# Chunk work of VectorE ahead of a step's maximum in the first cross-attention, and the added one of the silu on ScalarE

## The chip, the core and the metric

The kernel runs on one core of a Trainium2 chip. The metric is the device time of one execution in microseconds (us). Engines: TensorE (PE; its weight loads are shown as PEld), VectorE (DVE), ScalarE (ACT), GpSimd (POOL), SyncE (SP), which issues the DMAs. Each engine takes its instructions strictly in the order in which they are written; engines wait for each other on semaphores.

## What is computed

A decoder of two layers over x of 4 x 1024 x 256: self-attention, cross-attention to 154 context rows and a feed-forward network in each, every one with a residual and a layer norm behind it. The change lies in the stretch that computes the cross-attention of layer 0 and, beside it, the front half of layer 0's feed-forward for two of the four batch entries:

```python
# cross-attention of layer 0: 16 heads of 64
q = (Q @ Wq.T + bq).reshape(n, lq, H, D);  k, v likewise from the context
scores = jnp.einsum('nqhd,nkhd->nqkh', q, k) / jnp.sqrt(jnp.float32(D))
attn = jax.nn.softmax(scores, axis=2)
out = jnp.einsum('nqkh,nkhd->nqhd', attn, v)
x = _layernorm(x + out @ Wo.T + bo)
# feed-forward of layer 0
h = bit_linear(x, w1)                       # rows scaled and rounded
h = depthwise_conv1d(h.transpose(0, 2, 1), conv_w, conv_b)   # 3 taps
h = jax.nn.silu(h.transpose(0, 2, 1))
return bit_linear(h, w2)                    # needs each row's largest |h|
```

The silu is computed from the halved convolution c (taps and bias are halved ahead): silu = (tanh(c) + 1) * c.

## The kernel before

**Steps.** The cross-attention is a loop of 128 steps m. A step covers 128 query rows and 4 heads; four steps in a row (m mod 4 = 0, 1, 2, 3) share one set of queries. In this text r0, r1, r2, r3 name steps by m mod 4, and four steps from r3 to r2 are a group. In a step each engine does its part, in this order:

- TensorE: scores(m) into psA (L1025); transposes(m-2) of the normalised weights pr into psB (L1039 of four heads, L1041 of the rest), of which the first part waits until VectorE has copied out that of the step before; in r0 and r1 the queries of the next set; in r2 the output projection (16 matmuls, L978, wo_x); in r3 weights times values (L1056, L1061); and side work (transposing x, keys, values of the next entry) in some of the steps r0 and r1.
- VectorE: copy_transposes(m-3) (L1368, L1371), maxima(m) (L1377, waits for the scores), in r3 the residual (L1397, waits for the projection; TensorE's values wait for it), normalise_rows(m-1) (L1384, L1387, L1389), in r3 the statistics, in r0 the layer norm (L1409), and then the chunk work.
- ScalarE: the four exponentials of step m (L1242, wait for the maximum), its copies out of PSUM (queries L1183 in r0 and r1, values L1189 in r3), and then the chunk work.
- GpSimd: the inverse deviation (L1312, L1313), the bias of the next half (L1305, in every fourth r2), the rounding of x, and the chunk work.

**Chunks.** The hidden layer of 1024 features is done for two entries in 16 chunks of 128 features (128 partitions) x 1024 rows. Chunk i begins at step 61 + 4i, an r1: `chunk_from(m, n)` gives the chunk that began n steps before m. Its path through the engines before the change, with the steps behind its first (0 is r1, 1 is r2, 2 is r3, 3 is r0):

| offset | engine | operation | line |
|---|---|---|---|
| 0, 1 | TensorE | first layer, half 0 at the end of r1, half 1 within r2 | L978 |
| 0, 1 | VectorE | rescale of half 0, half 1, PSUM to hw | L1437 |
| 2 | ScalarE | outer_taps: the first tap into cvw, the third into yw | L1214, L1218 |
| 3 | VectorE | middle_tap, added to cvw | L1443 |
| 3 | GpSimd | add_tap: cvw = cvw + yw | L1290 |
| 5 | ScalarE | tanh of cvw into yw | L1222 |
| 5 | GpSimd | silu: yw = yw + 1, then yw = yw * cvw | L1294, L1295 |
| 7 | SyncE | store of yw to DRAM | L943 |
| 7 | ScalarE | absolute value into cvw | L1226 |
| 8 | VectorE | take_max: running maximum ymw over chunks, all 1024 columns | L1454 |

hw, cvw and yw have two buffers, so chunk i+2 takes those of chunk i. After each entry's last chunk ymw is transposed on TensorE (L1104, task ym) and reduced on VectorE (scale_hidden, L1462); for the second entry that stands at the end of the block. psO has two banks, given to TensorE's tasks in turn in the order in which they are written (C_SLOT).

## Time and profile before

| | us |
|---|---|
| median of 3 runs | 2543.93 |
| lowest and highest | 2537.71, 2546.5 |
| the profiled execution's own time | 2538.13 |
| its span, first to last instruction | 2536.2 |
| steps 0 to 60 (no chunk; steps by the start of their maximum) | 262.1 |
| steps 61 to 124 (16 groups, all with a chunk) | 364.5 |
| busy in the span: PE, DVE, ACT, POOL | 84%, 59%, 47%, 29% |

The whole span's shares mix stages with other limits. Only the stretch from 892 to 1564 us, the cross-attention, is touched, and of it mainly the 364.5 us with chunks.

### The profile page before, as it was taken

To read this page: it belongs to the slowest core of one execution; us is meant where nothing else is said; L and a number is where in the kernel's file an instruction comes from. 1 tells how busy PE (TensorE), PEld (TensorE's weight loads), DVE (VectorE), ACT (ScalarE), POOL (GpSimd) and SP (SyncE) were. 2 spreads that over 40 slices of the span, in tenths; PEclk is the share of its full clock that TensorE was granted. 3 is DMA by queue.
4 is the path that set the end of the run, shared out by engine and by line. 5 is a ranking of instruction groups with operands and counts; after the bars stand their busy time and mean duration, and the time that the engine had idled before them with its cause. 6 is when DMAs were issued, how large, how long until landed. Compare 5 with 4: busy or idle time off the path is not lost. (4 is left out here: it accounts for less than half of the span.)

```text
span 2536.2 us, 32771 instructions
## 1 busy us (share of the span) xinstructions
PE 2121.4 (84%) x11586; PEld 1190.8 (47%) x11586; DVE 1499.2 (59%) x2813; ACT 1180.7 (47%) x2629; POOL 740.4 (29%) x773
## 2 busy tenths in 40 slices
PE   6888888888888689998878875789899977788886
PEld 3333343344342345565555444556566643444444
DVE  5564565466564266666876885484836344557655
ACT  2345534534535255555655661466642314354342
POOL 4251310220010100122543444264723222343232
PEclk8899999999999899999999998999999978899898
DMA  7335333432421100001010003110001156544311
GB/s 158 98 55 139 75 63 74 89 73 59 69 46 43 62 20 5 26 26 34 32 46 24 32 32 139 61 40 9 28 13 62 36 115 121 114 94 88 71 54 42
DMA packets 132500, 156.56 MB, mean 62 GB/s; under 512 B 36477, under 2 KB 102913, under 8 KB 132242
## 3 DMA queue, kind: packets, MB, share of 16 engines
q1 hardware_dynamic: 132338, 154.47, 25.6%
q8 instruction: 94, 1.54, 0.3%
q14 instruction: 68, 0.56, 0.1%
HBM read 107.55 MB, written 46.86 MB: 61 GB/s over the span
## 5 line engine op out<-in xcount | busy, mean ns | idle before, releaser
L530 ACT ACTIVATE pbuf_sb<-psB 128x512 f32<-128x512 f32 (+1 forms) x608 | 331.0, 573 | 336.7 <-PE psB L409 312.9
L716 DVE TENSOR_REDUCE negm_sb<-psA 128x1 f32<-128x768 f32 (+6 forms) x352 | 347.1, 1022 | 136.8 <-PE psA L397 134.4
L1242 ACT ACTIVATE pw_sb<-psA,nmx_sb 128x154 f32<-128x154 f32 x512 | 192.4, 390 | 219.1 <-DVE nmx_sb L1377 219.0
L406 PE MATMUL psB<-qst_sb,kst_sb 99*128 99x512 bf16 (+3 forms) x768 | 235.1, 336 | 42.7 <-ACT pbuf_sb L530 34.6
L395 PE MATMUL psA<-kst_sb,qst_sb 96*128 96x512 bf16 (+3 forms) x768 | 200.5, 340 | 34.9 <-DVE negm_sb L716 29.9
L1377 DVE TENSOR_REDUCE nmx_sb<-psA 128x4 f32<-128x616 f32 x128 | 101.8, 795 | 142.5 <-PE psA L1025 142.5
L423 PE MATMUL psO<-pbuf_sb,V_sb 128*32 128x512 f32 (+3 forms) x1536 | 168.8, 513 | 8.8 <-ACT OT_sb L516 7.4
L406 PEld LDWEIGHTS psB<-qst_sb,kst_sb 99*128 99x128 bf16 x768 | 75.0, 99 | 180.7 <-ACT pbuf_sb L530 146.9
L2879 DVE TENSOR_REDUCE negm_sb<-psA 128x2 f32<-128x320 f32 x256 | 115.7, 480 | 71.0 <-PE psA L2646 65.9
L2766 ACT ACTIVATE pb_sb<-psB 128x512 f32<-128x512 f32 x160 | 92.8, 601 | 137.1 <-PE psB L2656 135.1
L1039 PE MATMUL psB<-ident_sb,pr_sb 128*128 128x128 f32 x512 | 85.0, 290 | 66.0 <-DVE pt_sb L1368 65.9
L395 PEld LDWEIGHTS psA<-kst_sb,qst_sb 96*128 96x128 bf16 x768 | 61.0, 100 | 159.4 <-DVE negm_sb L716 98.7
L2016 PE MATMUL psO<-va_sb,pat_sb 128*128 128x256 f32 x512 | 118.1, 384 | 9.9 <-DVE pat_sb L2446 9.9
L978 PE MATMUL psO<-XT_sb,wq_x_sb 128*128 128x512 f32 x256 | 124.2, 610 | 0.0
L978 PE MATMUL psO<-wo_x_sb,ox_sb 128*128 128x256 f32 x512 | 122.1, 395 | 2.0 <-DVE hw_sb L1437 1.2
L2646 PE MATMUL psA<-kst_sb,qst_sb 97*128 97x160 bf16 x512 | 83.3, 251 | 46.6 <-DVE negm_sb L2879 40.9
L1387 DVE TENSOR_TENSOR pr_sb<-pw_sb,prx_sb 128x512 f32<-128x512 f32 x128 | 118.3, 924 | 4.4
L2419 DVE TENSOR_REDUCE nma_sb<-psA 128x1 f32<-128x1024 f32 x32 | 39.1, 1222 | 138.2 <-PE psA L2016 138.2
L2016 PE MATMUL psA<-qa_sb,ka_sb 128*128 128x512 f32 x256 | 115.1, 592 | 0.0
L567 POOL TENSOR_TENSOR OT_sb<-OT_sb,rden_sb 128x1024 f32<-128x1024 f32 x15 | 35.3, 2354 | 270.9 <-DMA rden_sb<-dens_dram 270.9
L2016 PEld LDWEIGHTS psO<-va_sb,pat_sb 128*128 128x128 f32 x512 | 97.8, 192 | 33.8 <-DVE pat_sb L2446 13.8
L978 PEld LDWEIGHTS psO<-wo_x_sb,ox_sb 128*128 128x128 f32 x512 | 101.4, 200 | 19.5 <-issue 2.2
(308 smaller groups left out, 4495.9 us busy)
## 6 DMA issues: line engine op xcount, KB each, us to landing
qst_sb<-parts_dram SPq DMA_DIRECT2D x192, 128.0 KB, 4.6
rden_sb<-dens_dram SPq DMA_DIRECT2D x128, 128.0 KB, 2.7
parts_dram<-parts_sb SPq DMA_DIRECT2D x32, 384.0 KB, 3.1
kst_sb<-parts_dram SPq DMA_DIRECT2D x96, 128.0 KB, 7.5
x_dram<-X_sb SPq DMA_DIRECT2D x64, 128.0 KB, 1.7
y_dram<-yw_sb SPq DMA_DIRECT2D x16, 512.0 KB, 2.6
Y_sb<-y_dram SPq DMA_DIRECT2D x16, 512.0 KB, 8.4
parts_dram<-partsb_sb SPq DMA_DIRECT2D x16, 384.0 KB, 3.1
```

The lines of the kernel that those rows point to most:

```text
L395: nc.tensor.matmul(psA[:, k, at + lo:at + hi], qst[0:QK_ROWS, gg % 3, h, j * P:(j + 1) * P], kst[0:QK_ROWS, gg % 3, h, lo:hi], start=True, ...
L406: last = nc.tensor.matmul(psB[:, k, at:at + hi - lo], kst[0:MAX_ROWS, gg % 3, h, i * P:(i + 1) * P], qst[0:MAX_ROWS, gg % 3, h, lo:hi], st ...
L423: last = nc.tensor.matmul(psO[32 * h:32 * h + 32, c, lo - c * 512:hi - c * 512], V[:, b % 2, i, at:at + 32], pbuf[:, i % 2, h, lo:hi], sta ...
L530: nc.scalar.activation(pbuf[:, key % 2, heads[0]:heads[-1] + 1, lo:hi], psB[:, (nb.n - 1) % 2, 0:len(heads) * (hi - lo)] .rearrange("p (h ...
L716: nc.vector.tensor_reduce(out=negm[:, gg % 2, heads[0]:heads[-1] + 1, j], in_=psA[:, (na.n - 1) % 2, :].rearrange("p (h n) -> p h n", h=le ...
L978: last = nc.tensor.matmul(dst, lhsT(i), rhs(i), start=(i == 0), stop=(i == n - 1))
L1242: last = nc.scalar.activation(pw[:, m % 2, h, :], psA[:, m % 2, at:at + K], ACT.Exp, bias=nmx[:, m % 2, h:h + 1], accum_out=psx[:, m % 3, ...
L1377: nc.vector.tensor_reduce(out=nmx[:, m % 2, :].rearrange("p (b a) -> p a b", a=2), in_=psA[:, m % 2, :].rearrange("p (a n) -> p a n", a=2) ...
L1387: nc.vector.tensor_tensor(pr[:, q % 3, 0:4, :], pw[:, q % 2, :, 0:P], prx[:, q % 3, :].unsqueeze(2).broadcast_to([P, 4, P]), ALU.mult)
L2016: last = nc.tensor.matmul(dst, lhsT(i), rhs(i), start=(i == 0), stop=(i == n - 1))
L2766: nc.scalar.activation(pb1[:, v % 2, h, :], psB[:, (nb.n - 1) % 2, :], ACT.Exp).then_inc(b_free, 1)
L2879: nc.vector.tensor_reduce(out=negm1[:, gg % 2, 2 * half:2 * half + 2, j], in_=psA[:, 0, half * 512:half * 512 + 2 * KP].rearrange("p (a n) ...
```

## The change

On VectorE the chunk work stands between copy_transposes(m-3) and maxima(m) instead of at the step's end, one step later: the rescales at offsets 1 and 2, the middle tap at 4. take_max is split into halves of 512 columns, at offsets 9 and 11; each adds one to max_taken, so that the waits on it count double. On ScalarE outer_taps is split: first_tap stays at offset 2, last_tap goes to 3; tanh is followed by an Identity activation with a bias of one, which waits for the tanh by a semaphore; absolute goes to offset 8 and to the end of the step. On GpSimd add_tap goes to offset 4 and the silu is only the product. The store goes to 8. The transposes of the first entry's maxima go from step 99 to 101 and their reduction to step 102, ahead of its maximum. The second half of the very last take_max stands behind the last layer norm of the block. A tile `one` is set at the block's start.

```diff
@@ row_tasks
-        if part == 1 and spread_from(m, 38) is not None and spread_from(m, 38) < SPILL - 1:
-            out += [("ym", spread_from(m, 38), 0), ("ym", spread_from(m, 38), 1)]
+        if part == 1 and spread_from(m, 40) is not None and spread_from(m, 40) < SPILL - 1:
+            out += [("ym", spread_from(m, 40), 0), ("ym", spread_from(m, 40), 1)]
@@ sync
-                if chunk_from(m, 7) is not None:
-                    store_hidden(chunk_from(m, 7))
+                if chunk_from(m, 8) is not None:
+                    store_hidden(chunk_from(m, 8))
@@ tensor
-                pe.wait_ge(max_taken, FH * (f + 1))
+                pe.wait_ge(max_taken, 2 * FH * (f + 1))
@@ scalar
-            def outer_taps(i):
+            def first_tap(i):
                 c = i % FH
                 act.wait_ge(c_dve, C_FREED[("h", i, 1)])
-                act.wait_ge(w_halved, 2)
+                act.wait_ge(w_halved, 3)
                 if i >= 2:
-                    act.wait_ge(max_taken, i - 1)
+                    act.wait_ge(max_taken, 2 * (i - 1))
                 nc.scalar.activation(cvw[:, i % 2, :], hw[:, i % 2, 0:S], ACT.Identity, bias=hconvb[:, c:c + 1],
                                      scale=hconv[:, c, 0:1]).then_inc(conv0_made, 1)
+
+            def last_tap(i):
+                c = i % FH
                 if i >= 2:
                     act.wait_ge(w_stored[i % 2], 16 * (i // 2))
                 nc.scalar.activation(yw[:, i % 2, :], hw[:, i % 2, 2:S + 2], ACT.Copy, scale=hconv[:, c, 2:3]).then_inc(conv2_made, 1)
@@ tanh
                 nc.scalar.activation(yw[:, i % 2, :], cvw[:, i % 2, :], ACT.Tanh).then_inc(tanh_made, 1)
+                act.wait_ge(tanh_made, 2 * i + 1)
+                nc.scalar.activation(yw[:, i % 2, :], yw[:, i % 2, :], ACT.Identity, bias=one[:, 0:1]).then_inc(tanh_made, 1)
@@ gpsimd
-                pool.wait_ge(tanh_made, i + 1)
-                link(nc.gpsimd.tensor_scalar(yw[:, i % 2, :], yw[:, i % 2, :], 1.0, None, ALU.add))
+                pool.wait_ge(tanh_made, 2 * (i + 1))
                 nc.gpsimd.tensor_tensor(yw[:, i % 2, :], yw[:, i % 2, :], cvw[:, i % 2, :], ALU.mult).then_inc(silu_made, 1)
@@ vector
-            def take_max(i):
+            def take_max(i, n):
                 f, c = i // FH, i % FH
+                at = slice(n * 512, (n + 1) * 512)
                 dve.wait_ge(abs_made, i + 1)
...
+                    dve.wait_ge(max_taken, 2 * i)
+                    ins = nc.vector.tensor_tensor(ymw[:, at], ymw[:, at], cvw[:, i % 2, at], ALU.max)
                 ins.then_inc(max_taken, 1)
-                dve.wait_ge(max_taken, i + 1)
...
             normalise(NU - 1)
+            take_max(FH * SPILL - 1, 1)
             scale_hidden(SPILL - 1)
```

Where the moved lines put the instructions is shown by the order on the engines. VectorE before, from the start of a step r1 to the maximum of r2 (L1368 and L1371 the copies, L1377 the maximum, L1437 a rescale, L1454 take_max):

```order
L1368 COPY pt_sb<-psB 128x4x128
L1371 COPY ptr_sb<-psB 128x128
L1377 TENSOR_REDUCE nmx_sb<-psA 128x2x2
L1384 RECIPROCAL prx_sb<-psx_sb 128x4
L1387 TENSOR_TENSOR pr_sb<-pw_sb,prx_sb 128x512
L1389 TENSOR_TENSOR pr_sb<-pw_sb,prx_sb 128x4x26
L1437 TENSOR_TENSOR hw_sb<-psO,rw_sb 128x512
L1454 TENSOR_TENSOR ymw_sb<-ymw_sb,cvw_sb 128x1024
L1368 COPY pt_sb<-psB 128x4x128
L1371 COPY ptr_sb<-psB 128x128
L1377 TENSOR_REDUCE nmx_sb<-psA 128x2x2
```

VectorE after, the same two steps (L1377 and L1380 are now the copies, L1386 the maximum, L1452 the middle tap, L1446 a rescale, L1465 half of take_max):

```order
L1377 COPY pt_sb<-psB 128x4x128
L1380 COPY ptr_sb<-psB 128x128
L1452 SCALAR_TENSOR_TENSOR cvw_sb<-hw_sb,hconv_sb,cvw_sb 128x1024
L1386 TENSOR_REDUCE nmx_sb<-psA 128x2x2
L1393 RECIPROCAL prx_sb<-psx_sb 128x4
L1396 TENSOR_TENSOR pr_sb<-pw_sb,prx_sb 128x512
L1398 TENSOR_TENSOR pr_sb<-pw_sb,prx_sb 128x4x26
L1377 COPY pt_sb<-psB 128x4x128
L1380 COPY ptr_sb<-psB 128x128
L1446 TENSOR_TENSOR hw_sb<-psO,rw_sb 128x512
L1465 TENSOR_TENSOR ymw_sb<-ymw_sb,cvw_sb 128x512
L1386 TENSOR_REDUCE nmx_sb<-psA 128x2x2
```

Between the normalising of r1 and the copy of r2 nothing is left; the middle tap has come in ahead of the maximum of r1, and a rescale with half a take_max ahead of that of r2.

ScalarE before, from the tanh of a step r2 to the absolute value at the end of r0 (L1242 the exponentials, L1189 and L1183 copies, L1214 and L1218 the taps):

```order
L1222 ACTIVATE yw_sb<-cvw_sb 128x1024
L1242 ACTIVATE pw_sb,psx_sb<-psA,nmx_sb 128x154 x4
L1189 ACTIVATE ox_sb<-psO,bv_x_sb 128x512 x2
L1214 ACTIVATE cvw_sb<-hw_sb,hconvb_sb,hconv_sb 128x1024
L1218 ACTIVATE yw_sb<-hw_sb,hconv_sb 128x1024
L1242 ACTIVATE pw_sb,psx_sb<-psA,nmx_sb 128x154 x4
L1183 ACTIVATE qx_sb<-psO,bq_x_sb 128x512
L1226 ACTIVATE cvw_sb<-yw_sb 128x1024
```

ScalarE after, from the tanh of r2 to the absolute value, which now ends r1 (L1248 the exponentials, L1228 the added one, L1215 and L1222 the taps, L1232 the absolute value):

```order
L1226 ACTIVATE yw_sb<-cvw_sb 128x1024
L1228 ACTIVATE yw_sb<-yw_sb,one_sb 128x1024
L1248 ACTIVATE pw_sb,psx_sb<-psA,nmx_sb 128x154 x4
L1190 ACTIVATE ox_sb<-psO,bv_x_sb 128x512 x2
L1215 ACTIVATE cvw_sb<-hw_sb,hconvb_sb,hconv_sb 128x1024
L1248 ACTIVATE pw_sb,psx_sb<-psA,nmx_sb 128x154 x4
L1184 ACTIVATE qx_sb<-psO,bq_x_sb 128x512
L1222 ACTIVATE yw_sb<-hw_sb,hconv_sb 128x1024
L1248 ACTIVATE pw_sb,psx_sb<-psA,nmx_sb 128x154 x4
L1184 ACTIVATE qx_sb<-psO,bq_x_sb 128x512
L1232 ACTIVATE cvw_sb<-yw_sb 128x1024
```

The third tap has moved behind the exponentials and the query copy of r0, and every step has at most two activations of 1024 columns.

## Rows read from the trace of the kernel before

**Rows 1.** Windows: width; busy us (count) PE, PEld, DVE, ACT, POOL; clock; DMA

```profile
1051.60:1120.00 68.40, 65.32 (x378) 40.95 (x377) 47.82 (x118) 38.64 (x151) 11.98 (x19) 1.00 0.07 23
1415.57:1476.43 60.86, 49.68 (x276) 29.65 (x276) 51.96 (x98) 38.67 (x122) 24.86 (x16) 1.00 0.09 33
1154.13:1518.63 364.50, 299.43 (x1600) 182.16 (x1600) 280.29 (x543) 214.28 (x661) 149.60 (x100) 0.97 0.09 34
```

**Rows 2.** Waits in 1154.13 to 1518.63: total us, times, longest

```profile
DVE nmx_sb L1377 <- PE psA L1025: 61.4, 28, 3.9
...
PE psB L1039 <- DVE pt_sb L1368: 47.6, 35, 3.6
```

**Rows 3.** Timeline of TensorE, one group (r3 to r2): start, us, operation, idle before

```profile
1425.77 0.80 PE L1025 MATMUL psA<-kb_sb,qx_sb 64*128 64x154 f32 x8
...
1427.89 1.13 PE L1056 MATMUL psO<-ptr_sb,v0r_sb 64*128 64x512 f32 x4 [0.63 <-DVE X_sb L1397]
...
1431.88 0.63 PE L1039 MATMUL psB<-ident_sb,pr_sb 128*128 128x128 f32 x4 [0.26 <-DVE pt_sb L1368]
...
1435.89 0.63 PE L1039 MATMUL psB<-ident_sb,pr_sb 128*128 128x128 f32 x4 [0.83 <-DVE pt_sb L1368]
...
1441.51 0.63 PE L1039 MATMUL psB<-ident_sb,pr_sb 128*128 128x128 f32 x4 [2.01 <-DVE pt_sb L1368]
...
1446.06 0.40 PE L1025 MATMUL psA<-kb_sb,qx_sb 64*128 64x154 f32 x2
```

**Rows 4.** Timeline of VectorE in the same group

```profile
1427.86 2.55 DVE L1387 TENSOR_TENSOR pr_sb<-pw_sb,prx_sb 128x512 f32<-128x512 f32 x1
...
1431.85 0.79 DVE L1377 TENSOR_REDUCE nmx_sb<-psA 128x4 f32<-128x616 f32 x1
...
1433.87 1.28 DVE L1443 SCALAR_TENSOR_TENSOR cvw_sb<-hw_sb,hconv_sb,cvw_sb 128x1024 f32<-128x1024 f32 x1
1435.06 0.68 DVE L1368 COPY pt_sb<-psB 128x512 f32<-128x512 f32 x1
...
1435.86 0.79 DVE L1377 TENSOR_REDUCE nmx_sb<-psA 128x4 f32<-128x616 f32 x1
...
1436.77 1.37 DVE L1387 TENSOR_TENSOR pr_sb<-pw_sb,prx_sb 128x512 f32<-128x512 f32 x1
...
1438.82 0.69 DVE L1437 TENSOR_TENSOR hw_sb<-psO,rw_sb 128x512 f32<-128x512 f32 x1 [0.51 <-PE psO L978]
...
1440.67 0.69 DVE L1368 COPY pt_sb<-psB 128x512 f32<-128x512 f32 x1
```

**Rows 5.** Timeline of GpSimd in the same group: the silu's product, the added tap

```profile
1427.51 2.36 POOL L1295 TENSOR_TENSOR yw_sb<-yw_sb,cvw_sb 128x1024 f32<-128x1024 f32 x1
...
1435.22 2.36 POOL L1290 TENSOR_TENSOR cvw_sb<-cvw_sb,yw_sb 128x1024 f32<-128x1024 f32 x1 [3.12 <-DVE cvw_sb L1443]
```

**Rows 6.** Group by form, VectorE, steps 0 to 60: busy us, mean ns, idle before

```profile
L1387 DVE TENSOR_TENSOR pr_sb<-pw_sb,prx_sb 128x512 f32<-128x512 f32 x60 | 42.6, 711 | 2.0
```

**Rows 7.** Timeline of ScalarE in the group: first tap; first exponential and tanh of r2

```profile
1431.52 1.23 ACT L1214 ACTIVATE cvw_sb<-hw_sb,hconvb_sb,hconv_sb 128x1024 f32<-128x1024 f32 x1
...
1442.30 0.39 ACT L1242 ACTIVATE pw_sb<-psA,nmx_sb 128x154 f32<-128x154 f32 x1 [3.23 <-DVE nmx_sb L1377]
...
1443.78 1.06 ACT L1222 ACTIVATE yw_sb<-cvw_sb 128x1024 f32<-128x1024 f32 x1
```

**Rows 8.** Group by form, ScalarE, steps 61 to 124

```profile
L1218 ACT ACTIVATE yw_sb<-hw_sb,hconv_sb 128x1024 f32<-128x1024 f32 x16 | 18.2, 1136 | 0.0
```

**Rows 9.** Timeline of VectorE where GpSimd adds the bias of the next half

```profile
1478.62 2.42 DVE L1389 TENSOR_TENSOR pr_sb<-pw_sb,prx_sb 128x104 f32<-128x104 f32 x1
```

**Rows 10.** Window at a slow output projection (r2), columns as in rows 1

```profile
1348.80:1354.00 5.20, 5.20 (x19) 4.02 (x17) 2.02 (x5) 2.21 (x9) 2.82 (x2) 0.70 0.02 3
```

**Rows 11.** Timeline at the end of the block

```profile
1559.26 0.63 PE L1104 MATMUL psO<-ident_sb,ymw_sb 128*128 128x128 f32 x4 [0.24 <-DVE X_sb L1397]
...
1560.84 0.41 DVE L1409 TENSOR_SCALAR X_sb<-X_sb,mv_sb,rstd_sb 128x256 f32<-128x256 f32 x1 [0.75 <-POOL rstd_sb L1313]
```

More of the change, by code:

```diff
@@ L776, in decoder_kernel @@
     hconvb = sb("hconvb", [P, FH], F32, second_stage)
+    one = sb("one", [P, 1], F32, second_stage)
     famw = sb("famw", [P, NT], F32, second_stage)
@@ L1322, in _ @@
             pool.wait_ge(w_halved, 2)
+            nc.gpsimd.memset(one[:, :], 1.0).then_inc(w_halved, 1)
+            pool.wait_ge(w_halved, 3)
             nc.gpsimd.memset(hw[:, :, 0:1], 0.0).then_inc(w_edges, 1)
@@ L1473, in _ @@
                     copy_transposes(m - 3)
+                if chunk_from(m, 1) is not None:
+                    rescale(chunk_from(m, 1), 0)
+                if chunk_from(m, 2) is not None:
+                    rescale(chunk_from(m, 2), 1)
+                if chunk_from(m, 4) is not None:
+                    middle_tap(chunk_from(m, 4))
+                if spread_from(m, 41) is not None and spread_from(m, 41) < SPILL - 1:
+                    scale_hidden(spread_from(m, 41))
+                if chunk_from(m, 9) is not None:
+                    take_max(chunk_from(m, 9), 0)
+                if chunk_from(m, 11) is not None:
+                    take_max(chunk_from(m, 11), 1)
                 if m < NM:
@@ L1499, in _ @@
                     scale_half(spread_from(m, -5), 1)
-                if spread_from(m, 38) is not None and spread_from(m, 38) < SPILL - 1:
-                    scale_hidden(spread_from(m, 38))
             for o in range(NU - G, NU):
```

23 lines of the change are left out of this document (8 added, 15 removed).

## The prediction

> **What bounds the kernel now.** I read the page first: no engine is full over the whole span, so the stretch that is changed has to be read alone. The windows give its state [rows 1]. Four groups without chunks take 68.40 us, and TensorE is busy 65.32 of them: it is the bound, idle 0.8 us a group. Three plain groups with a chunk (steps 105 to 116, no side work) take 60.86 us, 20.29 each, with TensorE busy 49.68, or 16.56 each: idle 3.73 us a group, at a granted clock of 1.00. VectorE is busy 51.96 there. Over all 16 groups TensorE is idle 364.50 - 299.43 = 65.1 us, 4.07 a group. These 65 us are all that the change can win, together with what a lower clock costs. Most of them are one wait: the transposes of a step wait 47.6 us for VectorE's copy of the step before, while VectorE itself stands 61.4 us idle ahead of its maximum, waiting for scores [rows 2]. So VectorE is late in some steps and early in others; that is what a reader should see first.
>
> The timeline of one plain group shows where [rows 3]: 0.63 before the values in r3 (they wait for the residual), then before the transposes 0.26 in r0, 0.83 in r1 and 2.01 in r2, together 3.73. The wait of r2 follows from VectorE's r1 [rows 4]: its maximum starts at 1435.86, the normalising L1387 takes 1.37 instead of the 0.69 to 0.71 it takes where GpSimd is quiet [rows 6], the rescale waits 0.51 for its matmul, take_max takes 1.2, and only then comes the copy, at 1440.67.
>
> **The lock.** L1387 was longer exactly where GpSimd ran. The added tap runs from 1435.22 to 1437.58 and L1387, begun at 1436.77, ends 0.56 behind that; the silu's product runs from 1427.51 to 1429.87 and L1387, begun at 1427.86, takes 2.55 and ends 0.54 behind it [rows 4, 5]. It did no work until GpSimd was done. The reductions out of PSUM under the same GpSimd instruction keep their 0.79 [rows 4]. By the Trainium skill ("SBUF — State Buffer", section "Who interferes with whom") a VectorE instruction with two inputs in SBUF and a GpSimd one that reads SBUF exclude each other for their whole length, whichever starts first winning; the trace agrees, 2.55 against 0.69. That rule speaks for a caution about this change: it moves work in time, and so moves who starts first.
>
> **The change part by part.** I lay one plain group out anew, with time 0 at the start of r2's transposes. TensorE alone, from rows 3: scores of r3 at 4.55 (1446.06 - 1441.51), transposes of r0 wanted 5.85 later at 10.40 (1431.88 - 0.26 - 1425.77, the 0.63 included), those of r1 3.18 after r0's (1435.89 - 0.83 - 1431.88), those of r2 3.61 after r1's (1441.51 - 2.01 - 1435.89). Sum 17.19, which is 16.56 + 0.63.
>
> *VectorE in r2.* The copy starts 0.84 ahead of the transposes it lets go (1440.67 and 1441.51), so at -0.84; the two copies take 0.80 (1435.06 to 1435.86). Rescale and half a take_max, 0.6 each, follow: r2's maximum at 1.2. Before, it would have been free at 0; the delay of 1.2 costs nothing, since TensorE is in its projection until 4.55.
>
> *ScalarE and the silu.* The exponentials of r2 start 0.83 behind the maximum's start, at 2.0; the tanh 1.48 later (1443.78 - 1442.30 [rows 7]), ending at 4.5. The added Identity is not in the trace; the nearest row is the third tap, 1.14 of the same shape with one operand per partition [rows 8]. I take 1.14, with 0.1 for each semaphore; it could not be under the tanh's 1.06 nor over the first tap's 1.23. The product starts at 5.9 and ends at 8.3. On GpSimd the removed instruction itself was off the path (that engine is busy 24.86 of 60.86 us [rows 1]); what counts is that the product now starts 0.7 ahead of L1387 of r3 (4.55 + 2.09 = 6.64), not 0.35 as before. L1387 is still blocked, and VectorE's copy for r0 comes 1.18 behind the product's end (before: maximum of r0 at 1431.85, less 0.80, less 1429.87), at 9.44. The transposes of r0 can start at 10.3: they wait 0 instead of 0.26.
>
> *r0.* Second half of take_max, done at 10.9; maximum at 10.9 (its scores are ready 0.4 earlier). The copy of r1 comes 2.02 later (1433.87 - 1431.85), at 12.9, since the middle tap no longer stands ahead of it. Transposes of r1 at 13.75 against 13.58 wanted: 0.17 instead of 0.83.
>
> *r1.* Copies 0.8, middle tap 1.19, maximum at 14.9; L1387 wants to start 0.91 later, at 15.8. The added tap needs the middle tap (ready at 15.0) and ScalarE's third tap. ScalarE's first tap must wait for the second half of take_max, at 10.95 where it would have come at 10.30 (1431.52 less 1431.62, plus 10.40); with 1.13 for it, 1.48 for exponentials, 0.6 for the query copy and 1.14 the third tap ends at 15.3. The added tap therefore runs from 15.35 to 17.7 and again blocks L1387, now by 1.9 instead of 0.68: the 0.8 us of copies no longer lie between. L1387 ends at 18.3, L1389 at 18.4, the copy starts at 18.35, and r2's transposes at 19.2, against 13.75 + 3.61 = 17.36 wanted: a wait of 1.8 instead of 2.01. So most of what is won by taking the rescale and take_max (with 0.51 of waiting) out of this place is given back to the lock.
>
> The group: idle 0.63 + 0 + 0.17 + 1.83 = 2.63 instead of 3.73, 19.2 instead of 20.29. GpSimd's small inverse deviation falls into the half of take_max in r0 and may block it for 0.2; I take 1.0 saved, so 16.0 in 16 groups. Against that: where GpSimd adds the bias of the next half right behind the added tap (4 groups), L1389 takes 2.42 instead of 0.26 [rows 9]; before, 0.51 of that lay under the rescale's wait, now none: 4 x 0.5 = 2.0. At the end of the block the last half of take_max (0.6), two sets of transposes (0.63 each) and their semaphores (0.2) now follow the last layer norm of 1560.84, where the reductions followed at once; one set lies under the first reduction: 1.5 [rows 11]. The moved scale_hidden is the same work once, ahead of a maximum instead of a copy: I take 0, between a loss and a gain of the longest waits seen, 3.6 and 3.9 [rows 2]. Setting `one` is one small write at the start under an idle GpSimd: 0. Sum: -16.0 + 2.0 + 1.5 = -12.5 us. The profiled execution took 2538.13 (2536.2 of span and 1.9 around it), 5.8 less than the median; 2538.13 - 12.5 = 2525.6 there, and with the median 2543.93 - 12.5 = 2531.4.
>
> **The rivals.** *Side groups gain more.* Over all groups the idle is 4.07, more than the plain groups' 3.73, and in five of the sixteen the projection behind a long wait ran slowly: 5.2 us at a granted clock of 0.70 in one of them [rows 10], so partly at the lower level of 1.2 GHz, where 5.2 x 0.70 = 3.6 would do at 1.00. If all groups fall to 2.63 of idle: 65.1 - 42.1 = 23.0, with at most 1.6 each for those five projections (8; I take 6), less 3.5: about -25, so 2519. For it: the waits before those projections shrink. Against: they hold side work whose place is unchanged. Chance 0.20. *The lock misses r1.* If the added tap started behind L1389, the wait of r2 would lose its 1.8: -1.8 x 16 more, so about 2503. It needs a third tap 1.5 us later than I have it. Chance 0.05.
>
> *The lock turns, nothing is won.* If ScalarE's third tap ends over 0.45 later (15.8 instead of 15.35), L1387 goes first and the added tap blocks L1389 for its whole 2.36: transposes of r2 at about 20.05, 0.2 saved a group, -3 + 3.5, so 2544. The first tap's wait on take_max makes that near. Chance 0.20. *Slower.* The same, and the silu's product starting 0.75 or more later than 5.9, behind the start of r3's L1387 (6.64): then L1389 of r3 is blocked too, the copy of r0 comes 0.95 later, and through r0 and r1 that delay reaches r2: 21.0 a group, +0.7 x 16 + 3.5 = +15, so 2559. It decides from those two points together, in most groups. Chance 0.10. That the change does not do what it says has no room: the order is fixed in the program.
>
> **How the numbers follow.** My forecast has 0.45: 2531, by itself from 2523 to 2540 (0.5 either way a group). The rivals have 0.20, 0.05, 0.20 and 0.10. The range 2512 to 2548 leaves out the miss and the slower case, 0.15, and a little of the edges. What a measurement can tell from no change is 0.3%, 7.6 us, so 2536.3 and 2551.6. Faster than that: 0.8 of the forecast's 0.45, the 0.20 and the 0.05, together 0.61, I say 0.62. Slower: 0.12. Between: 0.26.
>
> **What would show it.** In the profile after: TensorE's idle in the plain groups 2.6 us; the wait of transposes for the copy in r1 near 0.2, in r0 none, in r2 still 1.8; L1387 (then L1396) about 2.4 long in every r3 and 2.6 in every r1, its mean above the present one; VectorE's maximum of r3 still waiting for scores; ScalarE's exponentials waiting less; at the end 1.5 us between the last layer norm and the first reduction. The forecast is wrong if L1398 (the old L1389) is the one that is long, if ScalarE rather than VectorE is what the transposes wait for in turn, or if the maximum is late enough that scores wait for exponentials.

## The result, and the profile after

| | before | after |
|---|---|---|
| median of 5 runs, us | 2543.93 | 2520.91 |
| lowest and highest | 2535.62, 2547.61 | 2516.67, 2527.73 |
| ratio, 95% interval | | 0.991 (0.989 to 0.993) |
| profiled execution, its span | 2538.13, 2536.2 | 2516.67, 2514.9 |
| start to the first maximum of the block | 891.8 | 887.3 |
| steps 0 to 60 | 262.3 | 262.5 |
| steps 61 to 124, 16 groups | 364.51 | 341.16 |
| step 125 to the next block | 45.50 | 46.30 |
| the rest | 972.1 | 977.6 |

The kernel became 0.9% faster; its median lies 10 us below the 2531 that was forecast. (The 262.1 us for steps 0 to 60 in the table ahead of the change are 262.3 when they are counted from the first maximum.) The change doesn't touch the first and the last of these five stretches; over all traces of this study they lay between 887 and 899 and between 972 and 981, so a difference of 5 us in one of them is scatter. All of the gain lies in the 16 groups: 23.35 us, where the sum of the prediction had 16.0 - 2.0 = 14.0.

First the windows of the kernel after, as in [rows 1]: the three plain groups, and all 16. The columns are width; busy us (count) of PE, PEld, DVE, ACT, POOL; granted clock; DMA share; GB/s.

```profile
1391.02:1448.31 57.29, 49.75 (x278) 29.81 (x277) 53.61 (x101) 41.97 (x124) 16.44 (x12) 1.00 0.09 35
1149.85:1491.01 341.16, 296.60 (x1611) 181.51 (x1613) 293.98 (x558) 231.08 (x675) 109.26 (x84) 0.97 0.10 36
```

A plain group takes 57.29 / 3 = 19.10 instead of 20.29, TensorE is busy 16.58 of it as before, and idle 2.51 instead of 3.73. Over all 16 groups the idle fell from 65.1 to 44.6. The waits over the same stretch (us in total, times, longest), against [rows 2]:

```profile
ACT pw_sb L1248 <- DVE nmx_sb L1386: 76.0, 40, 5.5
...
DVE nmx_sb L1386 <- PE psA L1026: 40.9, 25, 7.0
...
PE psB L1040 <- DVE pt_sb L1377: 23.8, 17, 4.2
```

The transposes wait for VectorE's copy half as long (47.6 before), and VectorE for scores 20 us less. Now one plain group in the timeline, as in [rows 3 to 5], r1 to r0; the columns are start, us, engine and operation, and in brackets the idle time before it and who ended it:

```profile
1409.24 1.16 ACT L1222 ACTIVATE yw_sb<-hw_sb,hconv_sb 128x1024 f32<-128x1024 f32 x1
...
1410.54 2.35 POOL L1298 TENSOR_TENSOR cvw_sb<-cvw_sb,yw_sb 128x1024 f32<-128x1024 f32 x1 [5.02 <-ACT yw_sb L1222]
...
1410.79 2.65 DVE L1396 TENSOR_TENSOR pr_sb<-pw_sb,prx_sb 128x512 f32<-128x512 f32 x1
...
1414.36 0.63 PE L1040 MATMUL psB<-ident_sb,pr_sb 128*128 128x128 f32 x4 [2.04 <-DVE pt_sb L1377]
...
1418.93 1.15 ACT L1228 ACTIVATE yw_sb<-yw_sb,one_sb 128x1024 f32<-128x1024 f32 x1
...
1420.16 2.35 POOL L1302 TENSOR_TENSOR yw_sb<-yw_sb,cvw_sb 128x1024 f32<-128x1024 f32 x1 [7.27 <-ACT yw_sb L1228]
...
1421.01 2.05 DVE L1396 TENSOR_TENSOR pr_sb<-pw_sb,prx_sb 128x512 f32<-128x512 f32 x1
1421.03 1.13 PE L1057 MATMUL psO<-ptr_sb,v0r_sb 64*128 64x512 f32 x4 [0.63 <-DVE X_sb L1406]
...
1424.69 0.66 PE L1040 MATMUL psB<-ident_sb,pr_sb 128*128 128x128 f32 x4
...
1427.94 0.63 PE L1040 MATMUL psB<-ident_sb,pr_sb 128*128 128x128 f32 x4
```

This is the group that was laid out: the waits of r0 and r1 are gone, that of r3 stays at 0.63, and r2 still waits 2.04, because the added tap (1410.54) starts 0.25 us ahead of the normalising, which then needs 2.65 instead of 0.69. This text calls it a lock when one of the two engines holds the other's instruction up like this.

It is not so in all groups. The first normalising instruction of r1 (L1396) is held up in seven steps, 69, 73, 105, 109, 113, 117 and 121. In six others, 65, 81, 85, 93, 97 and 101, all with side work of TensorE, the added tap starts a little later and holds up the second (L1398); this is the turned lock of the prediction's third rival:

```profile
1254.18 0.69 DVE L1396 TENSOR_TENSOR pr_sb<-pw_sb,prx_sb 128x512 f32<-128x512 f32 x1
...
1254.50 2.58 POOL L1298 TENSOR_TENSOR cvw_sb<-cvw_sb,yw_sb 128x1024 f32<-128x1024 f32 x1 [5.58 <-ACT yw_sb L1222]
...
1254.79 2.42 DVE L1398 TENSOR_TENSOR pr_sb<-pw_sb,prx_sb 128x104 f32<-128x104 f32 x1
```

In steps 77 and 89 the added tap comes behind both. What else changed shows at two more places outside the plain groups. The worst is a group in which GpSimd adds the bias:

```profile
1449.22 2.65 DVE L1396 TENSOR_TENSOR pr_sb<-pw_sb,prx_sb 128x512 f32<-128x512 f32 x1
...
1451.28 2.79 POOL L1312 TENSOR_TENSOR X_sb<-X_sb,bo_x_sb 128x1024 f32<-128x1024 f32 x1
1451.79 2.40 DVE L1398 TENSOR_TENSOR pr_sb<-pw_sb,prx_sb 128x104 f32<-128x104 f32 x1
1454.94 1.09 PE L1040 MATMUL psB<-ident_sb,pr_sb 128*128 128x128 f32 x4 [4.18 <-DVE pt_sb L1377]
...
1456.89 5.42 PE L979 MATMUL psO<-wo_x_sb,ox_sb 128*128 128x256 f32 x16
```

Both normalising instructions are held up one after the other, TensorE waits 4.18, and the output projection behind it takes 5.42 instead of 3.6, at a granted clock of 0.66 (the window of it, columns as above):

```profile
1456.89:1462.31 5.42, 5.42 (x19) 4.22 (x17) 2.35 (x7) 3.69 (x10) 1.52 (x1) 0.66 0.00 0
```

And in the group from step 89, where GpSimd's tap comes late behind the rounding of the next weights, the lock falls on a half of the running maximum:

```profile
1299.39 2.35 POOL L1298 TENSOR_TENSOR cvw_sb<-cvw_sb,yw_sb 128x1024 f32<-128x1024 f32 x1
1299.59 2.70 DVE L1465 TENSOR_TENSOR ymw_sb<-ymw_sb,cvw_sb 128x512 f32<-128x512 f32 x1
...
1305.52 6.07 PE L979 MATMUL psO<-wo_x_sb,ox_sb 128*128 128x256 f32 x16 [4.51 <-DVE hw_sb L1446]
```

Group by group (each from the maximum of its step to that of four steps later), the difference to before:

| group from step | 61 | 65 | 69 | 73 | 77 | 81 | 85 | 89 | 93 | 97 | 101 | 105 | 109 | 113 | 117 | 121 |
|---|---|---|---|---|---|---|---|---|---|---|---|---|---|---|---|---|
| us | -0.9 | -0.8 | -1.6 | -1.8 | -3.2 | -3.4 | -1.5 | +2.3 | -3.8 | -7.9 | +2.2 | -1.4 | -1.1 | -1.1 | +1.9 | -1.4 |

### The profile page after: what moved, and what is told of

Read it like the earlier page. It is cut to its first block and busy times, and to the rows that moved or that the text cites. A ratio compares the mean times of both kernels' runs of the same rounds, so it can differ in the third digit from the quotient of the medians.

```text
span 2514.9 us, 32817 instructions
## 1 busy us (share of the span) xinstructions
PE 2112.4 (84%) x11586; PEld 1188.8 (47%) x11586; DVE 1520.8 (60%) x2829; ACT 1199.0 (48%) x2645; POOL 697.8 (28%) x758
## 5 line engine op out<-in xcount | busy, mean ns | idle before, releaser
L1248 ACT ACTIVATE pw_sb<-psA,nmx_sb 128x154 f32<-128x154 f32 x512 | 192.2, 388 | 170.1 <-DVE nmx_sb L1386 170.1
L1386 DVE TENSOR_REDUCE nmx_sb<-psA 128x4 f32<-128x616 f32 x128 | 101.7, 795 | 121.9 <-PE psA L1026 121.7
L1396 DVE TENSOR_TENSOR pr_sb<-pw_sb,prx_sb 128x512 f32<-128x512 f32 x128 | 118.4, 925 | 4.4
L979 PEld LDWEIGHTS psO<-wo_x_sb,ox_sb 128*128 128x128 f32 x512 | 101.0, 200 | 22.4 <-issue 5.2
```

The lines of the kernel that those rows point to most:

```text
L979: last = nc.tensor.matmul(dst, lhsT(i), rhs(i), start=(i == 0), stop=(i == n - 1))
L1248: last = nc.scalar.activation(pw[:, m % 2, h, :], psA[:, m % 2, at:at + K], ACT.Exp, bias=nmx[:, m % 2, h:h + 1], accum_out=psx[:, m % 3, ...
L1396: nc.vector.tensor_tensor(pr[:, q % 3, 0:4, :], pw[:, q % 2, :, 0:P], prx[:, q % 3, :].unsqueeze(2).broadcast_to([P, 4, P]), ALU.mult)
```

## The experiments

Two executions are compared by their stretch of 16 groups and by the plain groups from steps 105, 109 and 113, which one trace gives to 0.1 us; the medians carry the scatter of the untouched stretches as well. Line numbers shift by a few lines between kernels. All ratios are to the kernel before, measured on the same chip.

**Order alone.** What does the moved one bring? Everything as after, but the one added on GpSimd:

```diff
-                act.wait_ge(tanh_made, 2 * i + 1)
-                nc.scalar.activation(yw[:, i % 2, :], yw[:, i % 2, :], ACT.Identity, bias=one[:, 0:1]).then_inc(tanh_made, 1)
...
-                pool.wait_ge(tanh_made, 2 * (i + 1))
+                pool.wait_ge(tanh_made, i + 1)
+                link(nc.gpsimd.tensor_scalar(yw[:, i % 2, :], yw[:, i % 2, :], 1.0, None, ALU.add))
```

> The changed kernel with one part undone: the added one of the silu is done by GpSimd again, 2.79 us, ahead of the product; VectorE's new order and ScalarE's split taps stay. My theory (the lock between GpSimd and VectorE sets the copies): GpSimd's addition runs from about 4.6 to 7.4 us behind r2's transposes, so it blocks L1396 of r3 (wanted at 6.6), and the product behind it blocks L1398 until about 10.2; the copy of r0 then comes over 1 us late. Plain groups 20.2 to 20.8 us, so as slow as before the change (20.29), the whole about 2543 (-5 to +8 against before). Rival (the win is VectorE's order alone, GpSimd's addition is off the path as its 28% of busy time suggests): plain groups 19.2 as in the changed kernel, the whole about 2521.

Measured: 2519.7, ratio 0.992 (0.989 to 0.995); 16 groups 337.6, plain groups 18.8 to 19.0. My theory fell: the order alone brings the whole gain. (The 3.6 us that the 16 groups take less than in the kernel after go again from step 125 to the next block, 49.8 instead of 46.3.) The reason is in r3 (GpSimd and VectorE of this kernel):

```profile
1421.07 2.79 POOL L1300 TENSOR_SCALAR yw_sb<-yw_sb 128x1024 f32<-128x1024 f32 x1 [6.09 <-ACT yw_sb L1226]
...
1423.09 0.69 DVE L1395 TENSOR_TENSOR pr_sb<-pw_sb,prx_sb 128x512 f32<-128x512 f32 x1
...
1423.70 0.26 DVE L1397 TENSOR_TENSOR pr_sb<-pw_sb,prx_sb 128x104 f32<-128x104 f32 x1
...
1423.94 2.37 POOL L1301 TENSOR_TENSOR yw_sb<-yw_sb,cvw_sb 128x1024 f32<-128x1024 f32 x1
...
1425.22 1.64 DVE L1464 TENSOR_TENSOR ymw_sb<-ymw_sb,cvw_sb 128x512 f32<-128x512 f32 x1
```

The instruction that adds the one runs for 2.79 us, and the normalising, which begins 2.02 behind its start, takes 0.69: by then it holds nothing up (what it does earlier stands in the last section). The product behind it starts when the normalising is through and makes one half of the running maximum 0.95 longer, for which nobody waits. So with the one on GpSimd the product is late enough to miss the normalising; with the one on ScalarE it is early and hits it. Neither is worth anything against the other here that the times could tell. Which part of the order brings how much, the middle tap, the halves of the running maximum or ScalarE's split taps, no run separates; only the rescales were put back by themselves, below.

**The moved one alone**, in the order of before:

> The kernel before with the other part alone: the added one on ScalarE behind the tanh, all orders as before. My theory: the product starts 1.6 us earlier, at about 1425.9 in the old group's times, and ends at 1428.3, so L1387 of r3 is blocked 0.4 us instead of 1.86 and the 0.26 of wait in r0 goes; the waits of r1 and r2 stay nearly as they are. Plain groups 19.8 to 20.1 instead of 20.29, the whole 3 to 9 us faster than before. Rival (each part stands for itself and this one brings half of the 23 us): plain groups about 19.6, the whole 11 us faster. Other rival (ScalarE's added 1.15 us delays the exponentials of r3): groups 20.5, slower by 3.

Measured: 2548.3, ratio 1.0025 (0.9999 to 1.0051), median of 10; plain groups 20.11 for two of three, and 21.77 for one whose projection ran at the lower clock. It brings 0.2 a plain group, and nothing that the time shows; the median leans the other way. In the profiled execution the 16 groups took 367.7, with nine projections at the lower clock instead of five (11.5 us over 3.62 each, against 5.7).

**Holding back the added tap.** On the kernel after, one wait on GpSimd until the normalising of the step is through:

```diff
                 if chunk_from(m, 4) is not None:
+                    pool.wait_ge(pr_normed, m)
                     add_tap(chunk_from(m, 4))
```

> The changed kernel with one wait more on GpSimd: the added tap waits until VectorE has normalised the rows of its step r1 (semaphore pr_normed), so it cannot hold the shared port while L1396 and L1398 of r1 want it. Nothing is left out. My theory: L1396 of r1 takes 0.69 instead of 2.65, the 2.04 us of wait ahead of the transposes of r2 falls to 0 to 0.4, plain groups fall from 19.2 to 17.2 to 17.6, and the whole by 18 to 29 us against the changed kernel, to 2492 to 2503; the added tap now blocks half a take_max in r2, by about 1 us, which lies under the output projection. Rival (TensorE waits in r2 for something else as well, such as ScalarE's absolute value through take_max, so the lock only hides it): groups fall by less than 0.5, the whole to 2513 or more.

Measured: 2504.4, ratio 0.985 (0.982 to 0.988); 16 groups 326.9, plain groups 18.07, over the 17.2 to 17.6 that I expected. The wait of r2 is gone, but in r3 something new stands:

```profile
1399.26 0.69 DVE L1397 TENSOR_TENSOR pr_sb<-pw_sb,prx_sb 128x512 f32<-128x512 f32 x1
1399.41 2.76 POOL L1302 TENSOR_TENSOR yw_sb<-yw_sb,cvw_sb 128x1024 f32<-128x1024 f32 x1 [5.09 <-ACT yw_sb L1228]
1399.87 2.42 DVE L1399 TENSOR_TENSOR pr_sb<-pw_sb,prx_sb 128x104 f32<-128x104 f32 x1
...
1403.57 0.63 PE L1040 MATMUL psB<-ident_sb,pr_sb 128*128 128x128 f32 x4 [0.56 <-DVE pt_sb L1378]
```

With the chunk's own chain no earlier but r2 and r3 2 us earlier, the product now starts behind the first normalising instruction: that one stays at 0.69, GpSimd waits for it (2.76 instead of 2.35), and the second, a fifth of the size, is held up and takes 2.42. This is the turned lock again, in r3 instead of r1, and r0 waits 0.56 for it.

**Third tap later.** On the kernel after, the first 512 columns of the third tap are computed once more ahead of it, so that the added tap starts some 0.7 us later:

> The changed kernel with ScalarE's third tap made later: its first 512 columns are computed once more ahead of it, into the same place, about 0.75 us. This tests the rival of the forecast that the lock turns. My theory: the added tap, ready at 1411.3 instead of 1410.5 in the group's times, comes behind the start of L1396 of r1 (1410.8); L1396 takes 0.69 and L1398 is blocked for about 2.5 us, transposes of r2 wait 2.5 to 2.9 instead of 2.04, plain groups 19.7 to 20.0, the whole 6 to 12 us slower than the changed kernel. If a shared port slowed both engines instead of locking, both L1396 and L1398 would be somewhat long and the group would change by less than 0.2.

Measured: 2525.0, ratio 0.993 (0.990 to 0.996); 16 groups 343.6; plain groups 19.41 with the projection at full clock, 20.8 where it was at the lower. In r1 the lock turned in all three plain groups; the last of them:

```profile
1434.36 0.69 DVE L1399 TENSOR_TENSOR pr_sb<-pw_sb,prx_sb 128x512 f32<-128x512 f32 x1
1434.86 2.40 POOL L1301 TENSOR_TENSOR cvw_sb<-cvw_sb,yw_sb 128x1024 f32<-128x1024 f32 x1 [5.78 <-ACT yw_sb L1225]
1434.97 2.42 DVE L1401 TENSOR_TENSOR pr_sb<-pw_sb,prx_sb 128x104 f32<-128x104 f32 x1
...
1438.13 0.63 PE L1041 MATMUL psB<-ident_sb,pr_sb 128*128 128x128 f32 x4 [2.23 <-DVE pt_sb L1380]
```

With the turned lock r2 waits 2.04, 2.04 and 2.23 in the three, against 2.04, and the one group at full clock takes 0.2 more than 19.21, where the rival was priced at 0.85 (20.1 a group). It would have been a small loss, not the end of the gain.

**What holds VectorE up?** The added tap replaced by an instruction that only writes; the sum of the taps is left out:

```diff
-                nc.gpsimd.tensor_tensor(cvw[:, i % 2, :], cvw[:, i % 2, :], yw[:, i % 2, :], ALU.add).then_inc(conv_made, 1)
+                nc.gpsimd.memset(cvw[:, i % 2, :], 0.5).then_inc(conv_made, 1)
```

> The changed kernel with the added tap on GpSimd replaced by an instruction that fills the same 1024 columns of the sum with a constant: it writes SBUF but reads none of it. The first and third taps of ScalarE and the middle tap are still computed, their sum is left out. Theory (what blocks VectorE is a GpSimd instruction that reads two arrays from SBUF, as the product and the added tap do, since the sum with an immediate did not block it in the run with order alone): the long normalising instruction of r1 is 0.69 again, the wait of r2 falls from 2.0 to 0.2, and the plain groups from 19.2 to 17.4, while the product still blocks r3. The median then lies near 2492. Rival (any long GpSimd instruction on the same buffers blocks, writes included): the normalising stays over 2 us in r1 if the fill takes as long as the tap, groups 19.2, 2521.

Measured: 2498.4, ratio 0.982 (0.979 to 0.986); 16 groups 318.5, plain groups 18.07.

```profile
1399.88 0.95 POOL L1298 MEMSET cvw_sb<- 128x1024 f32 x1 [5.00 <-ACT yw_sb L1222]
...
1400.15 0.69 DVE L1396 TENSOR_TENSOR pr_sb<-pw_sb,prx_sb 128x512 f32<-128x512 f32 x1
```

The fill starts 0.27 ahead of the normalising, as the tap did, and lies over it, and the normalising takes 0.69. It is shorter than the tap (0.95), but a lock by it would still have added 0.7. The 18.07 instead of the 17.4 that I expected is the turned lock of r3 again (wait of r0 0.57): I had forgotten that what frees r1 moves r3.

**All three held back.** Waits for the added tap, for the product (until the normalising of its step) and for the bias:

```diff
+                    pool.wait_ge(pr_normed, m)
                     add_tap(chunk_from(m, 4))
...
+                    pool.wait_ge(pr_normed, m + 1)
                     silu(chunk_from(m, 5))
...
+                    if h > 0:
+                        pool.wait_ge(pr_normed, m)
                     add_bias(h)
```

> The changed kernel with three added waits on GpSimd: added tap behind the normalising of its step, silu's product behind the normalising of its own step (r3), bias addition of the next half behind a normalising as well. Theory: no GpSimd instruction with two SBUF inputs then starts ahead of a normalising, so both of its instructions are 0.69 and 0.26 long in every step; the product falls on the half of the running maximum in r0, which starts 1 us before its maximum is wanted, so some 0.3 us may be lost there. Plain groups 17.4 to 17.7 instead of 18.07 with the tap alone held back, the stretch of 16 groups 316 to 320 instead of 326.9, median near 2496. Rival (the product lies in the way wherever it is put: the half of the running maximum is blocked for its whole length and r0 comes late by over 0.6): groups stay at 18.1 or more, 2504.

Measured: 2493.9, ratio 0.981 (0.977 to 0.984); 16 groups 315.1, plain groups 17.07, better than the 17.4 to 17.7 expected. The product costs one half of the running maximum 1.0 us, and nobody waits for it:

```profile
1426.60 2.36 POOL L1302 TENSOR_TENSOR yw_sb<-yw_sb,cvw_sb 128x1024 f32<-128x1024 f32 x1 [5.97 <-DVE pr_sb L1402]
...
1427.77 1.73 DVE L1469 TENSOR_TENSOR ymw_sb<-ymw_sb,cvw_sb 128x512 f32<-128x512 f32 x1
```

TensorE's only wait in the group is the 0.63 for the residual.

**Order alone, with tap and bias held back:**

> The changed order with the silu's added one on GpSimd as in the kernel before, and the added tap and the bias addition held back by a wait each until the normalising is through. Theory: the added one works as a delay that blocks nothing, so the product starts behind the normalising of r3 without a wait of its own; r3 and r1 are both free of the lock. Plain groups 17.3 to 17.7, the stretch 316 to 320, median near 2495, as with all three waits. Rival (the added one on GpSimd pushes the product so far that the absolute value and with it the running maximum of the chunk come late): groups over 18.1 and VectorE waiting over 1 us for the absolute value.

Measured: 2509.6, ratio 0.986 (0.981 to 0.990); 16 groups 324.0, plain groups 17.85. The rival was nearer, though by another way than it said:

```profile
1435.70 2.36 POOL L1301 TENSOR_TENSOR yw_sb<-yw_sb,cvw_sb 128x1024 f32<-128x1024 f32 x1
...
1435.98 2.62 DVE L1467 TENSOR_TENSOR ymw_sb<-ymw_sb,cvw_sb 128x512 f32<-128x512 f32 x1
...
1441.37 0.63 PE L1040 MATMUL psB<-ident_sb,pr_sb 128*128 128x128 f32 x4 [0.62 <-DVE pt_sb L1379]
```

Here the product, which no wait holds back, starts 0.28 ahead of the half maximum instead of 1.17, makes it 1.9 longer, and r0's maximum and r1's transposes come 0.62 late. So the one on ScalarE is worth 17.85 - 17.07 = 0.8 a group once the locks are out of the way, and nothing as long as they are there.

**Rescales back.** On the kernel after, both rescales at the end of their steps as before:

```diff
-                if chunk_from(m, 1) is not None:
-                    rescale(chunk_from(m, 1), 0)
-                if chunk_from(m, 2) is not None:
-                    rescale(chunk_from(m, 2), 1)
...
                     copy_value_rest(*side[1:])
+                if chunk_from(m, 0) is not None:
+                    rescale(chunk_from(m, 0), 0)
+                if chunk_from(m, 1) is not None:
+                    rescale(chunk_from(m, 1), 1)
```

> The changed kernel with both rescales of the hidden back at the end of their steps, as before, and everything else as after: the middle tap, the halves of the running maximum, the maxima's scaling, ScalarE's order and the added one unchanged. Theory (part of the gain comes from taking the first rescale out from between the normalising of r1 and the copy that lets r2's transposes go; its wait of 0.51 for a matmul lies under the lock now): the wait of r2 grows by one rescale, 2.0 to 2.7, plain groups 19.9, 16 x 0.7 = 11 us, median 2532. Rival (the whole gain comes from the running maximum in halves and the middle tap): 19.2 and 2521.

Measured: 2538.5, ratio 0.9985 (0.996 to 1.001), and yet two of the three plain groups took 19.19; the third (20.85) ran in part at the lower clock (0.92 over the group). So in the plain groups the rival was right: a wait of 2.08 instead of 2.04. Some 0.3 of the rescale's 0.6 is hidden since the normalising comes later against the tap (0.59 behind its start instead of 0.25) and is held up for less; the rest goes into slack that VectorE has in r0, where its maximum waits 0.2 to 1.0 for the scores in the plain groups, as it doesn't in those of the kernel after. The lock:

```profile
1450.86 2.35 POOL L1298 TENSOR_TENSOR cvw_sb<-cvw_sb,yw_sb 128x1024 f32<-128x1024 f32 x1 [5.76 <-ACT yw_sb L1222]
...
1451.45 2.30 DVE L1396 TENSOR_TENSOR pr_sb<-pw_sb,prx_sb 128x512 f32<-128x512 f32 x1
...
1455.27 0.63 PE L1040 MATMUL psB<-ident_sb,pr_sb 128*128 128x128 f32 x4 [2.08 <-DVE pt_sb L1377]
```

The 12 us more over the 16 groups (353.3) are 6.9 of idle time of TensorE and 5.2 of busy time, at a granted clock of 0.96 instead of 0.97. Much of it lies in groups with side work: the one from 85 took 26.7 instead of 22.4, with 1.4 more of idle time and a granted clock of 0.87 instead of 1.00. How much of the lower clock follows from the longer waits I can't say from this run.

**Rescales back, all held back:**

> The kernel with all three waits on GpSimd and both rescales back at the end of their steps. With the lock in place the rescale's old position cost nothing in the plain groups (19.19 against 19.21). Theory (the lock hid it, since the copy waited for GpSimd's tap anyway): with the lock gone it shows, plain groups 17.7 to 18.2 instead of 17.07 (0.6 of work, up to 0.5 of waiting for its matmul), and the median 10 to 17 above the kernel with three waits. Rival (the rescale's position is worth nothing at all): 17.1.

Measured: 2500.0, ratio 0.983 (0.980 to 0.986); 16 groups 323.8, plain groups 17.85. With the lock gone the same position costs 0.78 a plain group: 0.6 of work and 0.18 of waiting for its matmul. The lock had covered it.

**Step 89.** The kernel with all three waits, and the late added tap of step 89 held back one step more:

```diff
-                    pool.wait_ge(pr_normed, m)
+                    pool.wait_ge(pr_normed, m + 1 if spread_from(m - 1, -5) is not None else m)
```

> The kernel with all three waits on GpSimd, and the added tap of step 89, which comes late behind the quantising of the next weights, held back by one step more, behind the normalising of r2. Theory (in the group from 89 the added tap blocked the half of the running maximum for 2.69, so the maximum of r2 and with it the rescale that frees a bank for the output projection came 2 us late, the projection waited 4.5 and then ran 6.2 long): the wait falls to about 2.5, the projection to 3.6 to 5, the group from 28.9 to 24 to 26.5, all others stay; the median 2490, within 4 of the kernel with three waits. Rival (the wait for the bank is set by something else than the blocked half): the group stays at 28 or more.

Measured: 2492.0, ratio 0.980 (0.976 to 0.984); 16 groups 310.6, the group from 89 24.34 instead of 28.87, all others the same to 0.03.

```profile
1298.17 0.69 DVE L1469 TENSOR_TENSOR ymw_sb<-ymw_sb,cvw_sb 128x512 f32<-128x512 f32 x1
...
1302.10 3.69 PE L979 MATMUL psO<-wo_x_sb,ox_sb 128*128 128x256 f32 x16 [2.50 <-DVE hw_sb L1450]
```

2.0 us of lock on one instruction had cost 4.5: 2.0 of waiting and 2.5 of clock. This is the fastest version found, 2% under the kernel before. By form (busy us, mean ns), its two normalising instructions are at their unblocked lengths; the kernel after had 1119 and 562 ns:

```profile
L1400 DVE TENSOR_TENSOR pr_sb<-pw_sb,prx_sb 128x512 f32<-128x512 f32 x64 | 44.5, 695 | 2.2
...
L1402 DVE TENSOR_TENSOR pr_sb<-pw_sb,prx_sb 128x104 f32<-128x104 f32 x64 | 17.0, 265 | 0.0
```

**The maxima's scaling alone**, on the kernel before: `spread_from(m, 38)` becomes 40 for the transposes, and scale_hidden moves to the front of step 102.

> The kernel before with one part of the change alone: the transposes of the running maximum are numbered in step 101 instead of 99, and the scaling they feed runs at the front of step 102 instead of at the end of step 99. It happens once. The prediction gave it 0. Theory now (at the end of r3 VectorE waited 1.98 for those transposes, and the copy for r0 behind it came 2.03 late; in the trace after the two groups from steps 97 and 101 took 20.90 and 24.29 instead of 28.80 and 22.10): those two groups together take 45 to 46 instead of 50.9 and all others stay as before, stretch 359 instead of 364.5, median 5 to 6 under the kernel before. Rival (the gain of the group from 97 came from the rest of the order, and the scaling costs the same wherever it stands): the two groups together stay at 50 to 51.

Measured: 2540.6, ratio 0.999 (0.998 to 1.001), so not told apart from no change; the group from 97 took 24.18 instead of 28.80 and that from 101 22.59 instead of 22.10, together 4.1 less, a little short of the 5 to 6 expected. Only 1.0 of this is idle time of TensorE (9.1 in the two groups before, 8.0 here); 3.1 is busy time, at a granted clock of 0.93 and 1.00 instead of 0.88 and 0.92. Whether the moved scaling raised the clock is not shown: in the same two traces groups 85, 89 and 93, whose instructions are those of before in the same order, took 6.1 more, 3.0 of it in their projections at the lower clock, and groups 105, 117 and 121 another 4.3, so that the stretch was 370.4 and not 359. The wait itself, in the kernel before:

```profile
1384.59 0.69 DVE L1462 TENSOR_REDUCE famw_sb<-psO 128x4 f32<-128x512 f32 x1 [1.98 <-PE psO L1104]
...
1388.16 0.63 PE L1039 MATMUL psB<-ident_sb,pr_sb 128*128 128x128 f32 x4 [2.03 <-DVE pt_sb L1368]
```

VectorE stood 1.98 for the transposes of the maxima at the end of r3, with the copy for r0 behind it. With the scaling moved both waits are gone, and group 101 has 0.7 more of idle time.

## Why the prediction was right, and where it was not

The time lay within the range and the direction was right; the mechanism held in the plain groups, where it was worked out, and missed in the groups with side work and where a zero had been written. That the range held is partly luck: 2520.9 lies below the 2523 to 2540 that the forecast gave by itself, and the range reached it for the sake of the first rival; what the side groups won beyond the forecast stood against what groups 89, 101 and 117 lost.

- *The plain group* was right, 19.2 forecast and 19.10 measured: waits of 0.63, 0 and 0 (0.17 forecast), and 2.04 in two of three (1.83). Behind the added tap the normalising of r1 takes 2.65 (2.6), behind the product that of r3 2.05 (2.4). But the sixteen groups did not give 1.1 each, as the sum had it: they run from -7.9 to +2.3, and the 23 us are the sum of unlike parts.
- *"What counts is that the product now starts 0.7 ahead"*: it does (0.85, 1420.16 against 1421.01), but this failed as a reason. The step took the moved one as what removes the 0.26 of r0. In the order of before it does (that wait is gone in the run with the moved one alone, 0.2 a group); in the new order it is not needed: the run with order alone has the product 0.85 behind the normalising, and the same time. I had worked out only the group with the change, and never the same order with the one left on GpSimd. In that second layout the product falls on the half maximum, which has slack.
- *The moved scaling, "I take 0"*, failed. Its own row, the wait of 1.98 ahead of the first reduction, was in the trace before; I had looked only at the cost of the work, which is the same, not at what it waits for at either place. VectorE's wait and the 2.03 of TensorE behind it go with the move. In TensorE's idle time it is worth 1.0 by the run with it alone, in the time of the two groups 4.1 (5.7 between the two main traces); the difference is clock, and may be chance.
- *The bias, +2.0 for four groups*: each was to gain 1.0 and lose 0.5. The four, from 69, 85, 101 and 117, changed by -1.6, -1.5, +2.2 and +1.9. In the last both normalising instructions are held up, 2.65 and 2.40, and TensorE's idle time still fell by 0.6 (5.4 to 4.8), near the 0.5 forecast; its busy time rose from 16.6 to 19.0 at a granted clock of 0.86 over the group, where it was 1.00 before. The wait was sized rightly, the clock behind it was not in the sum.
- *The end of the block, +1.5*: from the last layer norm to the first reduction 0.33 became 1.76, so 1.4. The tail as a whole grew by 0.8 only.
- *The first rival, side groups gain more* (2519 at 0.20), is the nearest to the median of 2520.9. Groups 77, 81 and 93 gained 3.2 to 3.8 each, more than a plain group. Its first half came, more idle time saved: 20.5 us over all groups (it had 23.0). Its second half did not, fewer projections at the lower clock: these add up to 5.7 us over 3.62 each before and 5.2 after, only in other groups. The three groups show where the idle time went. Before, the copy that lets r2's transposes go stood behind a rescale that waited 1.08, 1.81 and 0.83 for its matmul (0.51 in a plain group), and behind take_max; the one of group 81:

```profile
1269.73 0.69 DVE L1437 TENSOR_TENSOR hw_sb<-psO,rw_sb 128x512 f32<-128x512 f32 x1 [1.81 <-PE psO L978]
```

Both are gone from that place, and with them the wait of r2: 2.86, 2.00 and 2.06 before, 0.17, none and none after, though in 81 and 93 the lock turned. Their idle time fell by 2.3, 2.3 and 2.1; besides, the projections of 81 and 93 ran at full clock now and took 1.7 and 1.6 less.

- *The lock turns*: in the plain groups it didn't, the margin held (the added tap came 0.25 ahead). In six groups with side work it did turn, and in two the tap missed the normalising, which the second rival had at 0.05 for all; the layout of the plain group had stood for these too. Made to turn in the plain groups, it costs 0.2 a group instead of 0.85, since the second normalising instruction is short and ends 0.13 behind GpSimd's, where the first ends 0.55 behind it with the second still to come.
- *The signs*: the waits of the plain group, VectorE's maximum of r3 waiting for scores (1.05) and ScalarE's exponentials waiting less (76.0 us instead of 122.3) came. One failed: the mean of L1396 did not rise (1119 ns against 1115 for L1387). And one that was to speak against the forecast came in part: L1398 is long in the groups with the turned lock, 562 ns on average against 366 for L1389.

The account for the 10 us between forecast and median: 9.4 in the 16 groups (23.35 against 14.0) and 0.7 at the block's end. In the 16 groups TensorE's idle time fell by 20.5 and its busy time by 2.8. Beyond 1.0 a group, 3.6 us of idle time went in groups 77, 81 and 93 and 3.1 in group 97, where the scaling had stood; group 89 lost 1.4. Five of the 16 projections ran at the lower clock before, three after.

## What to carry to other kernels

When instructions are moved on two engines that hold each other up, lay out both versions to a tenth of a microsecond, for each kind of group and not for the plain one alone, and ask for each long GpSimd instruction which VectorE instruction it meets and how much slack that one has: a lock on work with 1 us to spare cost nothing here, the same lock ahead of TensorE cost 2 us. Waits that keep GpSimd back until the urgent instruction is through won 16.5 us with one and 27 us with three of them; the whole reordering had won 23. Never write a zero for work that is moved unchanged: look up what it waits for at its old place and at its new one. A cost that vanishes under a lock (the rescale, the one on ScalarE) is not gone; it comes back as soon as the lock is removed, so such choices have to be tried again afterwards.
